# First layer's routed experts: 60 lots of 256 rows and 15 of 128, in order and unrolled, in place of a loop over 72 lots of 256

## The reference, cut to what matters

```python
def _L0_ffn_ref(x, Wr1, br1, Wr2, br2, Ws1, bs1, Ws2, bs2, We1, be1, We2, be2):
    I, E, K = 512, 8, 2
    xf = x.reshape(-1, Cc)                      # 8192 x 128
    logits = jax.nn.relu(xf @ Wr1 + br1) @ Wr2 + br2
    gates = jax.nn.softmax(logits, axis=-1)
    tg, ti = jax.lax.top_k(gates, K)
    tg = jax.nn.softmax(tg / K, axis=-1)
    out = jax.nn.silu(xf @ Ws1 + bs1) @ Ws2 + bs2
    for e in range(E):
        h = jax.nn.silu(xf @ We1[e] + be1[e]) @ We2[e] + be2[e]
        w = jnp.sum(tg * (ti == e), axis=-1)
        out = out + w[:, None] * h
    return out.reshape(Bb, Tt, Cc)
...
xn = _layernorm(x, axis=-1)
x = x + _L0_attn_ref(xn, ...) + _L0_ffn_ref(xn, ...)
xn = _layernorm(x, axis=-1)
x = x + _L1_attn_ref(xn, ...) + _L1_ffn_ref(xn, ...)
```

## Time and profile before

| | us |
|---|---|
| median of three runs | 1256.83 |
| the profiled execution, its own time | 1254.92 |
| its span, first to last instruction | 1253.2 |
| stage `first` | 0 to 100 |
| stage `attention` | 100 to 467 |
| stage `grouped` | 467 to 760 |
| stage `shared_and_last` | 760 to 1253 |

### The profile page before, as it was taken

One profiled execution on the slowest core, in us unless ns is written; L12 is line 12 of the kernel. 1 busy time (PEld: TensorE's weight loads), 2 busy tenths in 40 slices (PEclk: granted clock), 3 DMA queues, 4 the chain that ended last, 5 costly groups with the idle time before them and its releaser, 6 DMA issues. The chain is left out here.

```text
span 1253.2 us, 26697 instructions
## 1 busy us (share of the span) xinstructions
PE 1130.6 (90%) x9306; PEld 814.1 (65%) x9306; DVE 889.6 (71%) x2636; ACT 648.8 (52%) x1056; POOL 734.2 (59%) x908
## 2 busy tenths in 40 slices
PE   3963999999999969999999998999869899899994
PEld 2642555555555538999999896777646667667773
DVE  8986888888888746666666564888774489874442
ACT  4840777777777744444444344655523265553331
POOL 3204787777878754555555452334438567638886
PEclk9965999999999989999999998999889999999998
DMA  9904000000000012222222213122248312265543
GB/s 326 363 0 183 24 27 26 28 28 26 26 28 26 28 41 58 68 70 72 68 70 68 65 56 115 52 68 78 91 139 248 110 43 71 78 209 88 71 54 30
DMA packets 96813, 104.07 MB, mean 83 GB/s; under 512 B 12812, under 2 KB 84300, under 8 KB 96588
## 3 DMA queue, kind: packets, MB, share of 16 engines
q1 hardware_dynamic: 75792, 75.10, 19.5%
q0 software_dynamic: 19968, 26.63, 9.0%
q10 hardware_dynamic: 956, 1.04, 0.3%
HBM read 55.58 MB, written 47.15 MB: 82 GB/s over the span
## 5 line engine op out<-in xcount | busy, mean ns | idle before, releaser
L833 ACT ACTIVATE probs<-ps 128x1024 f32<-128x1024 f32 x256 | 254.5, 1025 | 110.2 <-PE ps L742 107.0
L1035 POOL DMA_INDIRECT slots<-rowbuf,slots x192 | 204.5, 1065 | 62.2 <-issue 36.3
L1146 POOL DMA_INDIRECT y<-slot_y,where x144 | 150.9, 1048 | 145.3 <-DVE slot_y L1127 121.7
L1214 ACT ACTIVATE slot_h<-ps,own 128x256 f32<-128x256 f32 x288 | 120.3, 470 | 153.7 <-PE ps L1178 152.0
L1178 PE MATMUL ps<-slot_x,own 128*128 128x256 f32 x576 | 141.1, 389 | 3.4 <-DVE slot_x L1116 2.9
L1190 PEld LDWEIGHTS ps<-own,slot_h 128*128 128x128 f32 x1152 | 140.4, 192 | 3.9 <-ACT slot_h L1214 0.2
L759 PE MATMUL ps<-probs,vext 128*32 128x256 f32 x2048 | 138.2, 388 | 3.1 <-issue 3.1
L1190 PE MATMUL ps<-own,slot_h 128*128 128x128 f32 x1152 | 140.6, 276 | 0.0
L1695 ACT ACTIVATE h<-ps,packs 128x512 f32<-128x512 f32 x128 | 85.5, 685 | 86.3 <-PE ps L1523 83.6
L1523 PE MATMUL ps<-xT,packs 128*128 128x512 f32 x256 | 119.1, 603 | 11.8 <-ACT h L1695 11.8
L1178 PEld LDWEIGHTS ps<-slot_x,own 128*128 128x128 f32 x576 | 105.2, 193 | 19.9 <-DVE slot_x L1116 8.0
(11 more groups left out here) (299 smaller groups left out, 2221.4 us busy)
## 6 DMA issues: line engine op xcount, KB each, us to landing
toeplitz<-conv_kernel SPq DMA_DIRECT2D x16, 1024.0 KB, 7.4
slots<-blank SPq DMA_DIRECT2D x26, 528.0 KB, 11.7
slot_rows<-slots SPq DMA_DIRECT2D x72, 132.0 KB, 2.2
routed<-y SPq DMA_DIRECT2D x32, 256.0 KB, 3.2
packs<-in_experts SPq DMA_DIRECT2D x1, 4624.0 KB, 14.5
packs<-in_experts SPq DMA_DIRECT2D x8, 578.0 KB, 6.8
xT<-slots SPq DMA_DIRECT2D x16, 264.0 KB, 2.8
stream<-in_x SPq DMA_DIRECT2D x8, 512.0 KB, 7.6
```

What stands on the lines that cost most here:

```text
L833: act.activation(probs[:, p % 4, :, :, :].rearrange("p j k t -> p j (k t)"), ps[:, 2 * (p % 2):2 * (p % 2) + 2, :], ACT.Exp, scale=DK ** - ...
L1035: return pool.indirect_dma_start(m["slot_dram"][layer], bass.IndirectOffsetOnAxis(ap=where, axis=0), m["rowbuf"][:, tile, :], None)
L1146: pool.indirect_dma_start(m["y_dram"][layer], bass.IndirectOffsetOnAxis(ap=where[:, j, h:h + 1], axis=0), y[:, j, h, :], None).then_inc(se ...
L1214: ins = act.activation(hidden[:, j % 2, k, :], ps[:, 2 * (j % 2) + k // 2, (k % 2) * LOT:(k % 2) * LOT + LOT], act_func, bias=own[:, j, P_ ...
```

## The change

The rows of an expert are rounded up to 128 instead of 256. With 16384 pairs and 8 experts that makes at most 135 pieces of 128. They are served by 60 whole lots of 256 and 15 half lots of 128: each expert takes as many whole lots as its number of pieces has pairs, and a half lot for an odd one; pairs of pieces that find no whole lot left go to half lots as well. The 75 lots are taken in turn, every fifth of them a half lot, and all of it is written out, without a loop.

```diff
-LOTS = (2 * TOKENS // LOT + E, TOKENS // LOT)
+WHOLE = 2 * TOKENS // LOT - E // 2
+HALF_LOTS = 2 * (2 * TOKENS // LOT - WHOLE) + E - 1
+STEPS = WHOLE + HALF_LOTS
...
-def staggered(engine, steps, count=GROUPS, buffers=2):
...
-    with engine.Fori(0, (count - peeled) // buffers) as r:
...
+def staggered(steps):
+    for i in range(STEPS + max(lag for _, lag in steps)):
         for step, lag in steps:
...
+            if 0 <= i - lag < STEPS:
+                step(i - lag, (i - lag) % UNROLL)
+def is_half(t):
+    return t % 5 == 4
+def lot_of(t):
+    return WHOLE + t // 5 if is_half(t) else t - t // 5
...
-                c.link(ts(tmp, size, 1.0 / LOT, 0.5 - 0.5 / LOT, ALU.mult, ALU.add))
...
-                c.link(stt(place[:, :, :], start.unsqueeze(1).broadcast_to([P, TILES, E]),
-                           float(LOT), place[:, :, :], ALU.mult, ALU.add))
+                c.link(ts(tmp, size, 1.0 / P, 0.5 - 0.5 / P, ALU.mult, ALU.add))
...
+                c.link(ts(pairs, tmp, 0.5, -0.25, ALU.mult, ALU.add))
...
+                c.did(ts(far, end, end[:, E - 1:E], -float(LOT), ALU.subtract, ALU.mult))
...
+                c.link(tt(z[:, :, :], place[:, :, :], wide_e(pairs), ALU.is_ge))
+                c.did(tt(place[:, :, :], place[:, :, :], wide_e(start), ALU.add))
+                c.link(tt(z[:, :, :], z[:, :, :], wide_e(far), ALU.mult))
+                c.link(tt(place[:, :, :], place[:, :, :], z[:, :, :], ALU.add))
...
             def put_y(t, j):
+                n = halves(t)
...
-                for h in range(HALVES):
+                for h in range(n):
...
-                for h in range(HALVES):
+                for h in range(halves(t)):
                     pool.indirect_dma_start(
...
-                pool.wait_ge(sem[f"sent{j}"], t * (16 * HALVES // UNROLL)
-                             + 16 * HALVES // UNROLL * (UNROLL - j))
+                pool.wait_ge(sem[f"sent{j}"], passed(t + UNROLL))
...
             def make_hidden(t, j):
+                n = halves(t) * P
...
-                    ins = pe.matmul(ps[:, 2 * (j % 2) + k // 2, (k % 2) * LOT:(k % 2) * LOT + LOT],
-                                    own[:, j, P * k:P * k + P], xs[:, j % 2, :], start=True, stop=True)
+                    ins = pe.matmul(ps[:, 2 * (j % 2) + k // 2, (k % 2) * n:(k % 2) * n + n],
+                                    own[:, j, P * k:P * k + P], xs[:, j % 2, 0:n], start=True, stop=True)
```

More of the change, by code:

```diff
@@ L54 @@
 SPARE = 4
-BLANK_CHUNKS = [(i, k) for i in range(2) for k in range(LOTS[i] * LOT // (BLANK * P))]
+SLOT_ROWS = (-(-(WHOLE * LOT + HALF_LOTS * P) // (BLANK * P)) * BLANK * P, TOKENS)
+BLANK_CHUNKS = [(i, k) for i in range(2) for k in range(SLOT_ROWS[i] // (BLANK * P))]
 P_DOWN = INTER
@@ L159, in build @@
         slots = sb("slots", [P, 2, TILES], mybir.dt.int32)
[L160 to L165, removed]
+        table = sb("table", [P, STEPS])
+        table_int = sb("table_int", [P, STEPS], mybir.dt.int32)
+        slot_dram = [nc.dram_tensor(f"slots{i}", [(SLOT_ROWS[i] + i * TOKENS), ROW], F32).ap() for i in range(2)]
+        y_dram = [nc.dram_tensor(f"y{i}", [3 * TOKENS + SLOT_ROWS[i], D], F32).ap() for i in range(2)]
         kernel_dram = nc.dram_tensor("conv_kernel", [P, KPAD], F32).ap()
@@ L240, in first @@
         chosen = sb("chosen", [P, TILES, E])
-        lots = sb("lots", [P, 4, E])
+        lots = sb("lots", [P, 8, E])
         n = TILES * E
@@ L1042, in grouped @@
     ps, ident = m["ps"], m["ident"]
-    lots = LOTS[layer]
     act_func = (ACT.Silu, ACT.Gelu_apprx_tanh)[layer]
     HALVES = LOT // P
+    halves = lambda t: 1 if is_half(t) else HALVES
+    passed = lambda t: 16 * sum(halves(i) for i in range(t % UNROLL, t, UNROLL))
     with ExitStack() as ctx:
@@ L1069, in _, with rows_loaded @@
             sp.dma_start(nwb[:, :], a["nwb"]).then_inc(sem["loaded"], 16)
[L1070 to L1076, removed]
+            for t in range(STEPS):
+                j = t % UNROLL
+                lot = lot_of(t)
+                sp.wait_ge(sem["downed"], t + 1)
+                sp.wait_ge(sem["weight_ready"], t + 1)
+                if is_half(t):
+                    sp.dma_start(rows[:, j, 0, :], half_slots[:, lot - WHOLE, :]).then_inc(sem[f"rows{j}"], 16)
+                else:
+                    sp.dma_start(rows[:, j, :, :].rearrange("p h d -> p (h d)"), slots[:, lot, :])\
                       .then_inc(sem[f"rows{j}"], 16)
-        def rows_loaded(t, j):
-            return t * (16 // UNROLL) + (16 - 16 // UNROLL * j)
+        def rows_loaded(t):
+            return 16 * (t // UNROLL + 1)
         @block.vector
@@ L1135, in _ @@
             dve.wait_ge(m["packs_loaded"], 16 * (layer + 1))
-            staggered(dve, [(get_own, 0), (take_x, 0), (put_y, 2)], lots, UNROLL)
+            staggered([(get_own, 0), (take_x, 0), (put_y, 2)])
         @block.gpsimd
@@ L1150, in free @@
             def free(t, j):
-                pool.wait_ge(sem[f"sent{j}"], t * (16 * HALVES // UNROLL)
-                             + 16 * HALVES // UNROLL * (UNROLL - j))
+                pool.wait_ge(sem[f"sent{j}"], passed(t + UNROLL))
                 pool.sem_inc(sem["y_free"], 1)
-            staggered(pool, [(free, 2), (send, 0)], lots, UNROLL)
+            staggered([(free, 2), (send, 0)])
         @block.tensor
@@ L1164, in turn @@
             def turn(t, j):
-                pe.wait_ge(sem[f"rows{j}"], rows_loaded(t, j))
+                pe.wait_ge(sem[f"rows{j}"], rows_loaded(t))
                 pe.wait_ge(sem["x_ready"], t + 1)
-                for h in range(HALVES):
+                for h in range(halves(t)):
                     ins = pe.transpose(ps[:, 4 + j % 2, P * h:P * h + P], rows[:, j, h, 0:D], ident)
@@ L1192, in make_out @@
                 ins.then_inc(sem["downed"], 1)
-            staggered(pe, [(turn, 0), (make_hidden, 1), (make_out, 2)], lots, UNROLL)
+            staggered([(turn, 0), (make_hidden, 1), (make_out, 2)])
             pe.wait_ge(m["pack0_loaded"], 16)
@@ L2029, in constants @@
     c[:, C_LAG:C_LAG + 2 * LOW] = np.concatenate([down, LOW * down])
-    c[:, C_COUNT:C_COUNT + LOTS[0]] = np.arange(LOTS[0])
+    half = np.arange(HALF_LOTS)
+    c[:, C_COUNT:C_COUNT + STEPS] = np.concatenate([np.arange(WHOLE), WHOLE + half // 2])
+    c[:, C_HALF:C_HALF + HALF_LOTS] = 2 * WHOLE + half
     c[:, C_TOKEN:C_TOKEN + TILES] = np.arange(TILES) * P + np.arange(P)[:, None]
-    c[:, C_TABLE1:C_TABLE1 + LOTS[1]] = np.arange(LOTS[1]) * LOT // CAP
     c[:, C_MASK:C_MASK + P] = np.kron(np.eye(8), np.ones((LOW, LOW)))
```

89 lines of the change are left out of this document (50 added, 39 removed).

## The result

The changed kernel takes 1263.66 us, the median of four runs (1263.3 to 1266.07), beside 1257.12 us for the kernel before: the ratio is 1.0056, with a 95% interval of 1.0044 to 1.0069. Forecast were 1258.3 us and, as the likeliest case, no change to be measured; it is slower by about 6.5 us. The case that it fell into had a chance of 0.35. The time lies inside the range (1250 to 1264), by 0.3 us, but that is luck: a cost that the forecast had put at nothing, some 12 us, met waits that it had some 5 us too large.

A forecast was written before the change was run, and what follows sets the result against it. PE was taken as the bound, with the four-buffer ring of results just as tight; -16.7 + 22.3 - 6.3 - 0.5 + 2.7 = +1.5 on 1256.83 gave 1258.3 us, range 1250 to 1264.

The forecast's parts named there:

- The case that it fell into: Whole kernel: measurably slower, above the "same" band of 1254.3 to 1259.3 us; chance 0.35.
- PE's work, -16.7: PE in `grouped`: 12 whole lots fewer save 44.8 us, 15 half lots of 1.87 add 28.1.
- the ring: Four result buffers, `put_y` through POOL's sends to DVE's `first` and `take_x`: two PE passes need 7.29 us, before 7.59.
- Waits at the half lots, +22.3: PE behind 14 half lots: two short passes last 5.70 us where the ring needs 7.29, so 1.59 each.
- Rival A: `grouped`: the ring gives way, few waits form, up to all 22.3 us go, giving 1236.0; chance 0.13.
- rival B: First sends of lots h - 3 and h - 2: ring keeps 7.59, sends stay late, +4.2 us, 1262.5; chance 0.20.
- Loop, -6.3: `grouped` written out: 17 branches back and register steps go, saving 6.3 of 6.5 us; bounds -6.5 and -5.0.
- the written-out code itself costs: Sign in `grouped` that the forecast is wrong: whole PE passes longer than 3.8 us.
- Pause, -0.5: POOL's one pause in `grouped`, worth 3.8 us, mostly stays: 0.5 us saved; bounds 0 and -3.8.
- Rival C: `grouped`: POOL's pause goes (-3.3) and the ring is at its short end (-1.3), 1253.7 us; chance 0.08.
- End of `first`, +2.7: DVE's longer `place_two` and table chain, no longer hidden by SP's stores, delays the next stage 2.7 us; bounds 1.9 and 3.4.
- Rival D, the clock: PE in `grouped`: its clock falls at repeated waits, about +25 us, 1283; chance 0.07.

The follow-up runs named there:

- 8: The changed kernel with eight result buffers instead of four and the rows of a lot loaded early: 1238.62 us, ratio 0.9872 to the kernel before.
- 9: The kernel before with its 72 whole lots all written out, no half lot, and eight result buffers: 1246.76 us, ratio 0.9941.
- 2: The kernel before, whole lots alone, with only PE's passes written out and the other engines in their loop: 1263.94 us, ratio 1.0052.
- 4: The changed kernel with its lots reordered, 60 whole ones first and then 15 half ones, all written out: 1259.77 us, ratio 1.0022.
- 5: The changed kernel with 60 whole lots first, 56 of them in a loop, then 15 half lots written out: 1253.11 us, ratio 0.9970.
- 7: The changed kernel with eight buffers instead of four for the results and their row numbers: 1239.49 us, ratio 0.9865.

## Why the prediction was wrong

**PE's work, -16.7: right.** With the ring out of the way (8 against 9) `grouped` takes 259.4 and 271.9 us: -12.4 for the half lots. The 4.3 that are missing are about 15 x 0.3: a round lasts 17.09 there, not 16.79, above all since pass h + 2 is 3.06 for 2.84, where PE's loading of weights waits some 0.2 us for DVE's `take_x` (15 times, 3.1 us, in 8).

**Waits at the half lots, +22.3: right in mechanism, too large.** The ring's way is 7.31 for 7.24, and its wait of 0.84 stands where it should, released by `take_x`, behind a wait of DVE for POOL's queue. The second was smaller, 0.09 in the best round. Both came to 1.18 there instead of 1.59, 13 x 0.41 = 5.3 us less in the 13 rounds. Rival A, that the waits do not form, is refuted by the same rows. So is rival B, whose 1262.5 lies nearest to the time: it needs two passes to last 7.59 and the copy to come as late as before, and the copy comes after 0.25 and the way is 7.31, not 7.54. Its number is near by chance.

**Loop, -6.3: this step failed.** It took nearly all of the 6.5 us as saved, and set nothing against the code that replaces the loop. In whole lots the saving is smaller: with all engines but PE written out the stage takes 278.3 for 281.7 us, 3.4, since every second or third pass is then 3.83, the ring's own wait of 0.1. And PE's written-out passes cost 7.5 by themselves (2), and 6.7 in equal lots (4 against 5), where the branches saved are already taken off. In the changed kernel the 13 rounds from 488.96 to 738.75 us are 13 x 1.24 = 16.2 over the best one; less 3.6 for the pause in one of them, 12.6 are left, and they stand beside the packets of PE's code (12.4 of them, see above). The prediction had named longer passes as a sign that "the written-out code itself costs", but gave this neither a term nor a chance. Both rows that could have warned were there: the page counts the code packets, and the kernel before has one, at 488.0 us, beside its first long pass.

**Pause, -0.5: right that it comes back.** It sits at the 242nd indirect DMA of the program in every kernel, at 696.98 us before and at 722.22 in the changed one, where POOL stands 2.01 ahead of the send:

```profile
722.22 0.96 POOL L1179 DMA_INDIRECT y<-slot_y,where  x1 [2.01 <-issue]
...
723.28 2.41 PE L1211 MATMUL ps<-slot_x,own 128*128 128x256 f32 x8 [2.24 <-DVE slot_x L1148]
```

Its pass lasts 6.59, its round 3.6 more than the best one. Rival C, that it goes, is refuted.

**End of `first`, +2.7: mechanism right, 1.7 measured.** DVE sets the barrier now, and its chain ends 3.6 later (101.44 for 97.81) where 4.5 was worked out. (Of the table's added steps three are with a wait and three without, not four and two; that is 0.1.)

**Rival D, the clock: in part.** The regular waits leave the granted clock at 1.00. In three rounds, the three longest, it falls for a while to the lower of its two levels (0.50, which is 1.2 GHz), each time behind two waits close together: 0.82 and 0.95 from 510 us on, 0.60 and 1.06 above, and 0.40 and 2.24 at POOL's pause. The first is the stretch from 507 us that is shown above with 0.86; the other two:

```profile
622.00:630.00 8.00, 6.34 (x30) 5.39 (x29) 4.18 (x16) 1.68 (x4) 3.58 (x4) 0.79 0.18 52
716.00:728.00 12.00, 9.36 (x59) 8.56 (x58) 6.51 (x25) 3.21 (x10) 5.65 (x6) 0.86 0.21 58
```

Each takes up to 1.7 us of PE at full speed (0.14 x 12, 0.21 x 8, 0.14 x 12), so of the 12.6 above up to 3.4 are the clock's, and of the pause 1.7. It makes the late landings dearer, and is no cost of its own: with eight buffers, where PE hardly waits, the granted clock is 1.00 from 480 to 735 us (7, 8 and 9).

**The sum.** For `grouped` -1.2 was forecast, 280.5 us, and 289.4 measured. The 8.9 between them is, in the 13 rounds, late landings with the clock behind them (+12.6), smaller waits (-5.3) and the pause (+0.3, 3.6 for 3.3); the +1.3 that is left stands in the stage's first 17.5 and last 22.1 us, and the runs do not divide it further.

What stays open: by which shared part a packet of code delays a row load or a send. The traces show that they overlap and land late, and the kernels show that PE's code is the cause; they do not show the path. Nor was the changed order of lots run with PE in a loop, so the 12.6 rest on where the time stands in one trace; what PE's code costs by comparison of times is known for whole lots alone, 6.7 and 7.5.

## What to carry to other kernels

Before less work is asked of the bounding engine, measure the slack of the next ring: here the half lots were worth nothing behind four result buffers and 8 us behind eight (1246.76 to 1238.62, with the rows loaded early), and the buffers alone were worth 8 to 10. Writing a loop out is not free even where the engine never waits for its code: here other transfers land late beside its packets, and a tight ring turns that into time. A wait that is taken away on one path (early rows) gives nothing while a second path of the same length stands beside it.

## What the runs showed of the hardware

- PE's code comes in packets of 16 KiB on queue 8, one for about five lots when written out (15 in the stage), one near the start of the stage in rounds of four lots, and three, all in its first 51 us, in rounds of eight. While one is under way, row loads of the changed kernel land after 2.81 us in the median instead of 2.06, and sends 2.35 behind POOL's end instead of 1.27. The other engines' packets of 8 KiB on queue 14 have no such cost: with 16 of them in the stage, and PE in its loop, the passes stay at 3.73 to 3.84 but for the first and the one at POOL's pause.
- POOL's pause of 1.8 to 2.0 us comes at the same indirect DMA of the program, the 242nd, in every kernel here. With eight buffers and whole lots PE does not feel it.
